# Ternary quantisation of the FFN weights moved from a stage of its own on ScalarE and VectorE into the first FFN tile, on GpSimd and VectorE

## The reference, cut to what matters

```python
# x: (4, 4096, 2048); each core has 2048 rows of one batch, and reads the batch's other 2048 for K and V
sq = elu(x @ Wq.T + bq) + 1 ; sk = elu(x @ Wk.T + bk) + 1 ; v = x @ Wv.T + bv
kv = einsum('bhsd,bhse->bhde', sk, v)
attn = einsum('bhsd,bhde->bhse', sq, kv) / (sq . sk.sum(axis=s) + 1e-6)
x = layernorm(x + attn @ Wo.T)

def absmean_quant(w):
    scale = mean(abs(w))
    return sign(w) * (abs(w) >= scale * 0.7)
h = gelu(x @ absmean_quant(w1).T + b1)        # w1: (8192, 2048)
x = layernorm(x + h @ absmean_quant(w2).T + b2)   # w2: (2048, 8192)
```

## Time and profile before

| | us |
|---|---|
| median of 3 runs | 5295.78 |
| the profiled execution | 5297.3 |
| its span (slowest core, core 1) | 5295.7 |
| spans of the 8 cores | 5250.9 to 5295.7 |
| granted TensorE clock, mean of the cores | 0.768 to 0.772 |
| PE busy | 2870.7 (54%) |
| ACT busy | 1586.5 (30%) |
| DVE busy | 1130.8 (21%) |
| POOL busy | 278.5 (5%), 518 instructions |

### The profile page before, as it was taken

The page is one execution under the profiler, slowest core; times in us unless marked ns, Lnnn a source line. Parts: engine busy times, 40 slices in busy tenths (PEclk is TensorE's granted clock), DMA queues, the critical chain, the costliest instruction groups (busy, mean ns, idle before and its releaser), DMA issues.

```text
span 5295.7 us, 39570 instructions; the slowest of 8 cores (5250.9 to 5295.7 us)
## 1 busy us (share of the span) xinstructions
PE 2870.7 (54%) x11722; PEld 1179.1 (22%) x11722; DVE 1130.8 (21%) x1976; ACT 1586.5 (30%) x1921; POOL 278.5 (5%) x518
## 2 busy tenths in 40 slices
PE   3972232222323232222222258995999599958996
PEld 1430110000101010000111013441344134423442
DVE  1431111112222221222222230014001500240023
ACT  0333333335555545555544411100110011001100
POOL 1000000000000001111111100000000000000000
PEclk9985665556666566666666669996999699979997
DMA  9544444543333335555544414443444344433442
GB/s 172 159 141 134 122 113 141 143 128 118 104 122 103 120 94 154 154 152 150 151 148 146 153 44 135 155 151 111 139 155 151 111 135 151 151 127 127 151 151 103
DMA packets 188072, 711.51 MB, mean 134 GB/s; under 512 B 24018, under 2 KB 28114, under 8 KB 171476
## 3 DMA queue, kind: packets, MB, share of 16 engines
q1 hardware_dynamic: 138676, 553.76, 33.0%
q0 software_dynamic: 49184, 155.22, 10.7%
HBM read 645.98 MB, written 100.66 MB: 141 GB/s over the span
## 4 chain that ended last, share of the span: by engine, by line
PE 41%; ACT 21%; DMA 19%; DVE 10%; issue 5%; POOL 1%; ACTq 1%; DVEq 1%; SPq 0%; POOLq 0%
PE PB L781 17%; PE PB L748 13%; DMA arnE<-w 8%; ACT arnC L305 5%; ACT arnC L308 5%; ACT arnC L313 5%; PE PB L477 5%; DMA arnC<-w1q 5%; DMA arnE<-xt 4%; DVE arnC L310 3%; ACT arnE L260 2%; PE PB L452 2%; PE PB L352 2%; PE PB L342 2%; ACT rows L449 1%
## 5 line engine op out<-in xcount | busy, mean ns | idle before, releaser
L748 PE MATMUL PB<-arnB,arnC 128*128 128x512 bf16 x4096 | 938.6, 385 | 261.6 <-DVE arnB L732 147.2
L781 PE MATMUL PB<-arnA,arnC 128*128 128x512 bf16 x4096 | 884.7, 379 | 0.0
L606 PE MATMUL PB<-arnB,arnC 128*128 128x512 bf16 x1024 | 275.3, 432 | 785.5 <-DVE arnE L621 785.3
L452 PE MATMUL PB<-rows,ones_k 1*128 1x512 f32 x128 | 96.4, 842 | 1060.2 <-ACT rows L449 1060.2
L748 PEld LDWEIGHTS PB<-arnB,arnC 128*128 128x128 bf16 x4096 | 391.9, 98 | 812.6 <-issue 384.1
L781 PEld LDWEIGHTS PB<-arnA,arnC 128*128 128x128 bf16 x4096 | 400.8, 98 | 483.3
L756 ACT ACTIVATE arnA<-PB,b_sb 128x512 bf16<-128x512 f32 x256 | 175.9, 687 | 802.6 <-PE PB L748 802.6
L790 DVE TENSOR_SCALAR arnE<-PB,b_sb 128x512 f32<-128x512 f32 x64 | 48.1, 751 | 1670.5 <-PE PB L781 1670.5
L260 ACT ACTIVATE arnE<-arnE 128x1024 bf16<-128x1024 f32 x256 | 270.4, 1056 | 432.2 <-DMA arnE<-w 340.1
L310 DVE TENSOR_TENSOR arnC<-arnC 128x1024 bf16<-128x1024 bf16 x256 | 177.3, 693 | 941.1 <-ACT arnC L308 940.3
L313 ACT ACTIVATE arnC<-arnC 128x1024 bf16<-128x1024 bf16 x256 | 270.4, 1056 | 280.9 <-DVE arnC L310 279.8
(11 more groups left out here) (149 smaller groups left out, 1798.4 us busy)
## 6 DMA issues: line engine op xcount, KB each, us to landing
arnE<-w SPq DMA_DIRECT2D x256, 512.0 KB, 4.2
arnC<-w SPq DMA_DIRECT2D x256, 512.0 KB, 3.9
arnC<-w1q SPq DMA_DIRECT2D x256, 512.0 KB, 3.4
arnC<-w2q SPq DMA_DIRECT2D x128, 1024.0 KB, 5.0
w1q<-arnC POOLq DMA_DIRECT2D x128, 256.0 KB, 2.6
w2q<-arnC POOLq DMA_DIRECT2D x128, 256.0 KB, 2.4
arnE<-xt POOLq DMA_DIRECT2D x64, 256.0 KB, 3.5
y1s<-arnE POOLq DMA_DIRECT2D x64, 256.0 KB, 2.4
```

The costliest lines, as they stand in the source:

```text
L452: e.matmul(o, l, r, start=True, stop=True),
L606: e.matmul(o, l, r, start=s, stop=z),
L748: e.matmul(o, l, r, start=s, stop=z),
L781: e.matmul(o, l, r, start=s, stop=z),
```

## The change

The quantisation jobs of the Q and Wo stages are removed. The weights are quantised in the first FFN tile (`t == 0`), directly into the buffers from which its matmuls read, and stored to `w1q` and `w2q` from there; tiles 1 to 3 load them from HBM as before. A piece is 128x512 now: 4 pieces for each of the 64 `w1` blocks, 8 for each of the 32 half blocks of `w2`, 512 in all. One piece is a load of 128x512 f32 (SP queue, four buffers), one comparison `w <= -T` on GpSimd into an f32 tile (two of them), one `(w >= T) - that` on DVE into the weight buffer, and a store on the POOL queue. The scale jobs are spread otherwise: 6 after each KV block (192), 8 after each of the first 8 heads (64). `gpsimd` joins `AUTO_CHAIN`, and the rows of the first layernorm are kept in other areas.

```diff
-    AUTO_CHAIN = ("vector", "scalar")
+    AUTO_CHAIN = ("vector", "scalar", "gpsimd")
...
-        emit_scale(2)
+        emit_scale(6)
...
-        emit_scale(24)
+        emit_scale(8)
...
-        emit_quant(12)
...
-        emit_quant(10)
-    while not qst["done"]:
-        emit_quant(8)
...
+    def quant_piece(which, idx, pc512, dst, dram_dst, dst_waits):
+        first = qres["rr"] == 0
+        sl = qres["rr"] % 4
+        bl = qres["rr"] % 2
+        qres["rr"] += 1
+        stage = Esl(5 + sl)
+        btile = Esl(9) if bl == 0 else Esl(2)
...
+        tok_d = dma("sync", stage, srcw,
+                    waits=[qres["stage_free"][sl],
+                           stats_guard if first else None])
+        tb = p.op("gpsimd", lambda e, o=btile, a=stage, b2=tneg:
+                  e.tensor_single_scalar(o, a, b2, ALU.is_le),
+                  waits=[tok_d, thr_done, qres["b_free"][bl],
+                         sqprev if first else None,
+                         abs_guard if first else None], inc=sP)
+        qres["lastB"] = tb
+        tqv = p.op("vector", lambda e, o=dst, a=stage, s2=tpos, b2=btile:
+                   e.scalar_tensor_tensor(o, a, s2, b2, ALU.is_ge, ALU.subtract),
+                   waits=[tb] + list(dst_waits), inc=sV)
+        qres["stage_free"][sl] = tqv
+        qres["b_free"][bl] = tqv
+        tw = dma("gpsimd", dram_dst, dst, waits=[tqv])
+        return tqv, tw
...
+            if t == 0:
+                wtoks = []
+                for pc in range(4):
+                    dw = [w1q_free[par]] + gwr_w1[par]
+                    if fc < 2:
+                        dw.append(last_q_mm[15])
+                    tqv, tw = quant_piece(
+                        "w1", fc, pc, buf[:, pc * 512:(pc + 1) * 512],
+                        w1q[fc, :, pc * 512:(pc + 1) * 512], dw)
+                    qres["wr_w1"][fc][pc] = tw
+                    wtoks.append(tw)
+                w1q_tok[par] = tqv
+                gwr_w1[par] = wtoks
+            else:
+                w1q_tok[par] = dma(
+                    "sync", buf, w1q[fc],
+                    waits=[w1q_free[par]] + qres["wr_w1"][fc] + gwr_w1[par])
+                gwr_w1[par] = []
...
+                if t == 0:
+                    wtoks = []
+                    for pc in range(8):
...
+                        tqv, tw = quant_piece(
+                            "w2", dc, hh * 8 + pc,
+                            sap[:, pc * 512:(pc + 1) * 512],
+                            w2q[dc, :, hh * 4096 + pc * 512:
+                                hh * 4096 + (pc + 1) * 512], dw)
...
+                    w2q_tok[slot] = tqv
```

More of the change, by code:

```diff
@@ L180, in build_nc @@
     sT = p.sem("sT", "tensor")
+    sP = p.sem("sP", "gpsimd")
     sV = p.sem("sV", "vector")
@@ L270, in emit_scale @@
             sst["done"] = True
[L272 to L323, removed]
@@ L636, in build_nc @@
                                  waits=[wo_mm_done])
-        emit_quant(10)
-    while not qst["done"]:
-        emit_quant(8)
     def Abc1(t):
-        return Ssl(t)
+        return Fst.ap()[:, (2 * t) * 512:(2 * t + 1) * 512] if t < 2 \
+            else Gfap[:, (2 * (t - 2)) * 512:(2 * (t - 2) + 1) * 512]
     def Bbc1(t):
-        return Sqsl(t)
+        return Fst.ap()[:, (2 * t + 1) * 512:(2 * t + 2) * 512] if t < 2 \
+            else Gfap[:, (2 * (t - 2) + 1) * 512:(2 * (t - 2) + 2) * 512]
     ab_done = [None] * NT
@@ L705, in build_nc @@
     out_last = None
-    quant_fence = [qst["lastC"], qst["lastV"], qst["qout"][0], qst["qout"][1],
-                   qst["stage"][0], qst["stage"][1]]
+    qres = {"rr": 0, "stage_free": [None] * 4, "b_free": [None, None],
+            "wr_w1": [[None] * 4 for _ in range(64)],
+            "wr_w2": [[None] * 16 for _ in range(16)], "lastB": None}
+    gwr_w1 = [[], []]
+    gwr_w2 = [[], [], []]
+    stats_guard = ab_done[3]
+    abs_guard = mx(sst["abs"][0], sst["abs"][1])
+    def quant_piece(which, idx, pc512, dst, dram_dst, dst_waits):
[5 more added lines that the diff above has]
+        btile = Esl(9) if bl == 0 else Esl(2)
+        if which == "w1":
+            srcw = w1[idx, :, pc512 * 512:(pc512 + 1) * 512]
+            tpos, tneg = thr.ap()[:, 1:2], thr.ap()[:, 0:1]
+        else:
+            srcw = w2[idx, :, pc512 * 512:(pc512 + 1) * 512]
+            tpos, tneg = thr.ap()[:, 3:4], thr.ap()[:, 2:3]
+        tok_d = dma("sync", stage, srcw,
[14 more added lines that the diff above has]
+        return tqv, tw
     def w1q_buf(i):
@@ L764, in build_nc @@
                 sap = w2q_slot(dc * 2 + hh)
[L765 to L770, removed]
+                if t == 0:
+                    wtoks = []
+                    for pc in range(8):
+                        dw = [w2q_free[slot]] + gwr_w2[slot]
+                        if dc < 2:
+                            dw.append(wo_mm_done)
+                        tqv, tw = quant_piece(
[3 more added lines that the diff above has]
+                                hh * 4096 + (pc + 1) * 512], dw)
+                        qres["wr_w2"][dc][hh * 8 + pc] = tw
+                        wtoks.append(tw)
+                    w2q_tok[slot] = tqv
+                    gwr_w2[slot] = wtoks
+                else:
+                    w2q_tok[slot] = dma(
+                        "sync", sap, w2q[dc, :, hh * 4096:(hh + 1) * 4096],
+                        waits=[w2q_free[slot]] + gwr_w2[slot]
+                              + qres["wr_w2"][dc][hh * 8: hh * 8 + 8])
+                    gwr_w2[slot] = []
                 halves.append((slot, sap, w2q_tok[slot]))
@@ L839, in build_nc @@
         tca = p.op("vector", lambda e, o=Esl(2), a=PB[4].ap():
-                   e.tensor_copy(o, a), waits=[tba], inc=sV)
+                   e.tensor_copy(o, a),
+                   waits=[tba, qres["lastB"] if t == 0 else None], inc=sV)
         tbb = p.op("tensor", lambda e, o=PB[4].ap(), l=ones_k1.ap(), r=row(2):
```

4 lines of the change are left out of this document (2 added, 2 removed).

## The result

The changed kernel is slower: 5854.81 us (median of 9 runs) against 5337.47 us (median of 10 runs of the kernel before on the same chip), ratio 1.0993, 95% interval 1.0925 to 1.1062. The forecast was 5374 us, with 5180 to 5600 as its range; the time lies above it. In some executions the cores of one die or both show a lower granted clock and take some per cent longer; the ratios here leave these out, and as cores 0 to 3 were such in the profiled execution of the changed kernel (up to 5941.3 us at clock 0.736), its rows are those of core 5 (5804.4 us at 0.760), beside core 1 of before (5295.7 us at 0.771).

The account below looks back on a forecast made before the run. Prediction: the long Q and Wo stages wait for weight work, while TensorE paces the KV stage and FFN. Terms 351 - 815 - 672 + 1213 = +77 us on 5297 us gave 5374 us, range 5180 to 5600.

Parts of the forecast that it names:

- the first term of the piece: Each quantised piece in the first FFN tile: GpSimd's 128x512 f32 comparison takes 0.93 us, of 2.95 us a piece.
- FFN tile 0: First FFN tile: 512 pieces at 2.95 us plus 175 us make 1685 us against 472, +1213 us.
- the upper bound of 1.5: GpSimd's comparison of a piece: at most 1.5 us, twice DVE's 0.75 us for L484.
- The mechanism itself: First FFN tile: comparison, DVE instruction and store of a piece run one after another, nothing of the next starting on GpSimd.
- the comparison on GpSimd is slow: First FFN tile, rival: at 1.5 us a comparison, a piece takes 3.52 us and the kernel 5666 us; chance 0.37.
- The second half's wait: First FFN tile, second half: pieces queue on DVE behind L799, 10.9 us more, 16 times, 175 us.
- KV and Q stages: KV: more scale jobs, +351 us, ending near 693 us; Q: fewer scale jobs and no quantisation, -815 us.
- 9.8 us every time: Q stage, within a head: the trace shows tiles 9.8 us apart without drift, held against a clock gain.
- The clock rival: Q stage: clock comes back once weight blocks are gone, 103 us saved on 60 tiles, 5271 us; chance 0.05.
- The Wo stage: Without quantisation: 48 x 5.8 + 15 x 7.5 = 392 us instead of 1065, -672 us.
- tiles 1 to 3: Later FFN tiles: they load weights as before, so they look as before.
- Loads: First FFN tile: covered, since four buffers give each three pieces, nearly 9 us, against a landing of 3.5 us.

Follow-up runs that it names:

- the copy kernel: Changed kernel with each piece's GpSimd comparison replaced by a plain f32 copy of the same size: 5309.45 us, ratio 1.0020 to the kernel before.
- the two further edits: On the changed kernel comparing on DVE: next block's pieces written ahead of the waiting instruction (4611.52 us), then half of w1 quantised between Q-stage tiles (4570.24 us, ratio 0.8643).

## Why the prediction was wrong, point by point

**The step that failed** is the first term of the piece in "FFN tile 0": "comparison on GpSimd, 128x512 f32: not in the trace ... I take 0.93". It measured 1.57 us, above even the upper bound of 1.5, and makes 512 x 0.64 = 328 us of tile 0's 431. The bounds came from DVE's rows and a one-column MEMSET, and neither says what GpSimd's loop costs; the trace before had no GpSimd arithmetic of any size. Of the other 103 us nearly all are small errors of the same kind: DVE's instruction 0.75 instead of 0.69 (a SCALAR_TENSOR_TENSOR with a pointer has the length of L484, not of L808), the store 0.59 instead of 0.54 and 0.04 before the next comparison (both only beside the tensor-scalar instruction: the copy kernel has 0.54 and nothing), less 0.02 at the first hop, together 0.13 us or 67 us; and the 33 us on the first pieces of buffers. The mechanism itself, and so the rival "the comparison on GpSimd is slow", was right: at 1.5 us it gave 5666 us, and 3.72 us a piece instead of 3.52 adds 102.

**The figure from the Trainium skill** ("GPSIMD Engine Reference", section "Performance versus the Vector engine"), 769 ns for 512 elements, is given there as the best case of a tight loop. By it the estimate was 5292 us, an error in the same direction as mine and larger. The copy's 622 ns is below it, the tensor-scalar's 1566 ns is twice it.

**The second half's wait** was right: 175 us forecast. The 512 pieces take 2103 us; less 511 x 3.72 and those 33 us that is 169 us for 15 passages, 11.3 us each against 10.9.

**KV and Q stages** were right: 676 us against 693, and 809 us against 808, with L433 mostly 9.8 us apart within a head as before. The prediction's "9.8 us every time" misreads the trace of before: on core 1 nearly half of the steps within a head take 10.1 to 11.8 us, the first of each head above all, and in the changed kernel such steps remain. The clock rival didn't come: the clock rose from 0.62 to 0.73 over the Q stage, but the tiles kept their 9.8 us. **The Wo stage** took 28 us more than worked out, most of it between blocks, where L568 starts 9.0 us apart on average and not the 7.5 that I had taken without a row, and **tiles 1 to 3** stayed as they were. **Loads** of pieces held up nothing in the changed kernel but the first (the 68.8 us in L677's row are one wait, ahead of the FFN).

**The chances** gave 0.42 to a forecast that hung on a single unmeasured number, at 51 us for each tenth of a microsecond, 0.37 to the slow comparison that came, and 5600 us as the end of a range whose own rival stood at 5666. The range didn't take in the bound that I had worked out.

## What to carry to other kernels

An instruction that moves to an engine on which nothing like it has been measured is the widest term of the sum, the more so inside a ring (steps that wait for each other in a circle) that is passed hundreds of times: measure it first. A store in the list of the engine that produces the next piece closes a ring of compute, hop, compute, hop and issue; another queue (here 14% off the kernel) or the same engine for both steps (19%) opens it. And a move may be a good one with the wrong engine in it: the same placement with DVE is 11% faster than the kernel before, and 14% with the two further edits.
